# Attention stage: in each of the twelve steps of a turn, TensorE's scores by key go ahead of its scores by query

## The chip, the cores and the metric

The kernel runs on one core of a Trainium2 chip. The time is device microseconds of that core for one execution, the median of several. Clocks of TensorE are given as the share of full speed that was granted.

## The reference

32 sequences of 256 tokens with 128 features go through half a feed-forward, a causal attention and another half feed-forward. The feed-forward is a mixture of eight experts of width 512; each token goes to its best expert if its rank there is below a capacity. What the change touches is the attention, whose core is:

```python
qkv = sn_dense(batch, W_qkv, u_qkv, sigma_qkv)           # 16 heads of 8 features
att = jnp.einsum('bhqd,bhkd->bhqk', q, k) * scale
att = jnp.where(causal[None, None] == 0, big_neg, att)
att = jax.nn.softmax(att, axis=-1)
x = jnp.einsum('bhqk,bhkd->bhqd', att, v)
x = x + sn_dense(x, W_proj, u_proj, sigma_proj)
```

(the residual is the layer's input). Behind it the router's affinities of the second feed-forward are worked out for the same sequence.

## The kernel before, in words

Five stages follow one another: token statistics, routing, experts, attention, experts. The attention (`attention`, from L1039) handles one sequence in a *turn* `b`, from b = -4 to 35, and each turn has NP = 12 *steps*, u = 0 to 11. Every engine walks the same turns and steps with its own list, and the engines are held together by semaphores alone. A sequence passes through several turns: its projections are made three turns ahead, its row maxima one and two turns ahead, its exponentials and outputs in its own turn, and normalisation, projection and the router's part one to four turns behind.

The softmax is made in two passes over the scores, and each step has a piece of both.

- *Scores by query* (`scores_by_query`, L1354 to L1369; called Q below): TensorE makes a 128 x 512 tile of scores with the query on the partitions, adds the causal mask by a matmul with the identity, and leaves it in one of two buffers `at_pp`. VectorE reduces the tile to row maxima (L1609, "the reduce"). Q of a step waits until the reduce of two tiles before is done. The tile belongs to a later sequence: `QUERY_TILES` (L1059) gives steps 0 to 4 the tiles 7 to 11 of sequence b+1 and steps 5 to 11 the tiles 0 to 6 of b+2. Tiles 0 to 3 are two matmuls of 256 columns (L1361) and a mask of 512 (L1363), the others one of 512 (L1366) and a mask of 256 (L1368).
- *Scores by key* (`scores_by_key`, L1371 to L1385; K below): TensorE makes the transposed scores of sequence b into one of two buffers `at_pm`, two matmuls of 256 columns (L1379) or, in every third step, four of 128 (L1383). The row maxima are subtracted within the matmul: they are extra rows of `qs`. ScalarE takes the exponential (L1291) and GpSimd zeroes what lies above the diagonal (L1207). K of a step waits until the exponential of two steps before is done, and K of step 0 also until the maxima have landed in `qs`.

The path of the maxima: after the reduce of tile 11 of sequence b+1 (step 4) GpSimd splits them into three bf16 pieces (L1259 to L1265, step 5), TensorE turns them (L1483, step 8), ScalarE copies them out (L1329) and SyncE's queue writes them into `qs` (L1169, `qs<-at_mt`); step 0 of the next turn uses them. In the same steps other transfers go out: VectorE's last split of the projections (L1642, step 5) is written to DRAM by SyncE's queue (L1164, `at_qkd<-at_part`) and read back by six transfers of ScalarE's queue (L1284, `qs<-at_qkd`, steps 9 to 11) and six of SyncE's (L1176, `kb<-at_qkd`), all of which wait for that write's landing (`part_out`).

On TensorE a step is Q, then K, then in every third step the product with the values (`times_v`, L1400, steps 0, 3, 6, 9), then `small(u)`: transposes and small matmuls. Those that matter below are in step 3 the transposes of `at_xn2` (L1415), which wait for VectorE's normalise of step 2 (L1582); in step 2 the q and k projections (L1418, L1419); in step 8 the turning of the maxima. VectorE's list has, beside one reduce in each step, in steps 10 to 2: two normalises of `at_xa` (L1582, step 10), statistics, the two `at_weight` operations (L1568, step 0), two `at_beats` (L1618, steps 0 and 1) and the two normalises of `at_x` (L1582, step 2).

Of the kernel before, what the change touches and what calls it, by code (L numbers as in the profile page):

```python
# [1038 lines left out]
def attention(nc, m, io, c, x_dram):  # L1039
# [9 lines left out]
    with ctx:  # L1049
# [81 lines left out]
        def wait(eng, s, n, most=None):  # L1131

            n = n if most is None else min(n, most)
            if n > 0:
                eng.wait_ge(s, n)

        def dma_count(b, slots, each=1):

            return lambda k: b * (16 * each // slots) + (16 * each - (k % slots) * (16 * each // slots))
# [210 lines left out]
        def _(pe):  # L1350
            te = nc.tensor

            def turn(b, k, has):
                def scores_by_query(o, v):  # L1354
                    n, s, out = b + o, (k + o) % NQ, pp[v % 2]
                    if v == 0:
                        wait(pe, qk_in[s], dma_count(n, NQ, 12)(s))
                    wait(pe, maxed, n * NP + (v - 1))
                    if v < 4:
                        for w in range(2):  # L1360
                            te.matmul(out[:, w * S:(w + 1) * S], qs[s][0:ROWS, 2 * v + w, 0:P], kb[s][0:ROWS, 2 * v + w, :, 0:P],  # L1361
                                      start=(w == 0), stop=False, skip_group_check=True)
                        te.matmul(out, c.identb[:, :], c.mask[:, :, :].rearrange("p a q -> p (a q)"),  # L1363
                                  start=False, stop=True, skip_group_check=True).then_inc(pre_done, 1)
                    else:
                        te.matmul(out, qs[s][0:ROWS, v - 4, P:S], kb[s][0:ROWS, v - 4, :, :].rearrange("p r q -> p (r q)"),  # L1366
                                  start=True, stop=False, skip_group_check=True)
                        te.matmul(out.rearrange("p (r q) -> p r q", r=2)[:, :, P:S], c.identb[:, :], c.mask[:, 0:2, :],  # L1368
                                  start=False, stop=True, skip_group_check=True).then_inc(pre_done, 1)  # L1369

                def scores_by_key(u):  # L1371
                    s, out, quad, w = k, pm[u % 2], u // 3, u % 3
                    g, r = 4 * (quad // 2), quad % 2
                    if u == 0:
                        wait(pe, m_in[s], dma_count(b, NQ)(s))
                    wait(pe, exped, b * NP + (u - 1))
                    if w < 2:
                        for i in range(2):
                            last = te.matmul(out[:, i * S:(i + 1) * S], kb[s][:, g + 2 * w + i, r, 0:P], qs[s][:, g + 2 * w + i, :],  # L1379
                                             start=True, stop=True)  # L1380
                    else:
                        for j in range(4):
                            last = te.matmul(out[:, j * P:(j + 1) * P], kb[s][:, g + j, r, P:S],  # L1383
                                             qs[s][:, g + j, P:S], start=True, stop=True)
                    last.then_inc(main_done, 1)  # L1385

                def times_v(n, s, quad):
                    half, r = quad // 2, quad % 2
                    out, values = po, vp[s][:, :, :, :].rearrange("p j h w -> p j (h w)")
                    if quad == 0:  # L1390
                        wait(pe, v_out, n + 1)
                        wait(pe, ot_out, n)
                    wait(pe, masked, n * NP + 3 * (quad + 1))
                    for w in range(3):
                        src = pt[3 * quad + w]
                        for i in range(2 if w < 2 else 4):
                            j = 2 * w + i if w < 2 else i
                            cols = S if w < 2 else P
                            at = 32 * (8 * half + 2 * j + r) - 16 * r
                            last = te.matmul(out[32 * j:32 * j + 32, (half + 1) * S - cols:(half + 1) * S],  # L1400
                                             values[:, w // 2, at:at + 32], src[:, i * cols:(i + 1) * cols],
                                             start=(w < 2 and r == 0), stop=(w == 2 and r == 1), skip_group_check=True)
                    last.then_inc(pv_done, 1)
# [81 lines left out]
                        last.then_inc(mt_tr, 1)  # L1485

                for u in range(NP):
                    for o, v in QUERY_TILES[u]:
                        if has(o):
                            scores_by_query(o, v)  # L1490
                    if has(0):
                        scores_by_key(u)
                    if u >= LAG and (u - LAG) % 3 == 2 and has(0):
                        times_v(b, k, (u - LAG) // 3)
                    if u < LAG and (u - LAG) % 3 == 2 and has(-1):
                        times_v(b - 1, (k - 1) % NQ, (NP - LAG + u) // 3)
                    small(u)

            run(turn)
            pe.wait_ge(seen, TPB * B)  # L1500
            te.matmul(ps_n, c.onesb[:, :], c.hots[B % 2][:, 3 * TPB, :], start=True, stop=True).then_inc(counted, 1)
# [245 lines left out]
```

## Time and profile before

| what | value |
|---|---|
| time, median of 3 runs | 1045.26 us (1042.62 to 1045.60) |
| time of the profiled execution | 1035.15 us |
| its span, first to last instruction | 1033.3 us |
| TensorE matmul busy, whole span | 896.4 us (87%) |
| VectorE busy | 724.8 us (70%) |
| ScalarE busy | 607.5 us (59%) |
| GpSimd busy | 682.8 us (66%) |
| TensorE clock granted, mean | 0.955 |

Shares over the whole span mix five stages, so they say little of the attention, which fills about 286 to 860 us of the span. How to read the rows below: a timeline row has start, duration, engine, line, operation, output and input, count, and in brackets the idle time of the engine before it and what ended that. A "q" behind an engine's name (SPq, ACTq) is its sequencer issuing DMAs. Ends of matmuls are modelled, so the distance between starts is what a matmul really takes of TensorE. A turn is recognised by its transposes L1415, one pair in each.

### The profile page before, as it was taken

The page shows a single profiled execution, that of the slowest core. Times are in us where ns is not written, and L with a number is a line of the kernel's source. Part 1 is how long each engine was busy: PE and PEld are TensorE (multiplying, and loading weights), DVE is VectorE, ACT ScalarE, POOL GpSimd, SP SyncE. Part 2 cuts the span into 40 slices and gives each one's busy share as a digit, 9 for nine tenths or more (in the row PEclk, how much of TensorE's full clock was granted, in tenths as well). Part 3 has the DMA queues.
Part 4 walks back from the last instruction along what each step waited for, and adds up shares of the span by engine and source line. Part 5 has one row for each costly group of instructions (what it writes and reads, how often), then busy time and mean ns, then how long its engine had stood idle before and what let it go on. Part 6 is the DMA issues. An engine that isn't in the chain of part 4 may idle for free. (4 is left out here: it accounts for less than half of the span.)

```text
span 1033.3 us, 26499 instructions
## 1 busy us (share of the span) xinstructions
PE 896.4 (87%) x8219; PEld 679.6 (66%) x8219; DVE 724.8 (70%) x2368; ACT 607.5 (59%) x1581; POOL 682.8 (66%) x1247
## 2 busy tenths in 40 slices
PE   5937499999647999999999999999999873999995
PEld 5823399999623566565656666565656542999995
DVE  8879745444237889899998989998898845444441
ACT  2637366666313666676666666666666651766662
POOL 7709668643023678888888888888887773355554
PEclk9999799999958999999999999999999985999998
DMA  7450022223145544446354554545454102222220
GB/s 214 128 173 1 17 69 67 69 66 64 40 79 106 122 96 101 115 94 122 95 116 101 109 108 97 121 95 117 95 115 97 39 24 61 60 67 67 64 59 21
DMA packets 127407, 89.72 MB, mean 87 GB/s; under 512 B 14305, under 2 KB 117910, under 8 KB 127270
## 3 DMA queue, kind: packets, MB, share of 16 engines
q1 hardware_dynamic: 103078, 52.69, 22.8%
q10 hardware_dynamic: 15488, 17.74, 7.7%
q0 software_dynamic: 8704, 17.60, 6.6%
q8 instruction: 70, 1.15, 0.5%
q14 instruction: 67, 0.55, 0.2%
HBM read 52.23 MB, written 35.47 MB: 85 GB/s over the span
## 5 line engine op out<-in xcount | busy, mean ns | idle before, releaser
L1291 ACT ACTIVATE at_pt<-at_pm 128x512 f32<-128x512 f32 x384 | 228.5, 598 | 117.9 <-PE at_pm L1379 84.2
L1609 DVE TENSOR_REDUCE at_mx<-at_pp 128x2 f32<-128x512 f32 (+1 forms) x384 | 259.5, 678 | 44.7 <-PE at_pp L1368 37.1
L1207 POOL TENSOR_SCALAR_AFFINE_SELECT at_pt<-at_pt 128x256 f32<-128x256 f32 (+1 forms) x384 | 187.8, 493 | 57.4 <-ACT at_pt L1291 54.1
L925 ACT ACTIVATE e_ht<-e_ps_h,b1t 128x128 f32<-128x128 f32 x576 | 164.8, 370 | 98.2 <-PE e_ps_h L954 98.2
L964 PE MATMUL e_ps_y<-w,e_ht 128*128 x1152 | 159.2, 282 | 0.0
L954 PE MATMUL e_ps_h<-e_xnt,e_w1own 128*128 128x128 f32 x1152 | 154.8, 279 | 1.4 <-issue 1.4
L954 PEld LDWEIGHTS e_ps_h<-e_xnt,e_w1own 128*128 128x128 f32 x1152 | 143.0, 195 | 1.6 <-issue 1.6
L964 PEld LDWEIGHTS e_ps_y<-w,e_ht 128*128 128x128 f32 x1152 | 140.0, 192 | 1.7
L1011 DVE SCALAR_TENSOR_TENSOR e_y<-e_ps_y,e_x 128x256 f32<-128x256 f32 x72 | 30.6, 425 | 155.7 <-PE e_ps_y L964 155.7
L888 POOL DMA_INDIRECT out_dram<-e_y,e_x x72 | 73.6, 1022 | 86.4 <-DVE e_y L1011 74.8
L1400 PE MATMUL at_po<-at_pt,vp 128*32 128x256 f32 (+1 forms) x2048 | 109.8, 332 | 1.6 <-POOL at_pt L1207 1.6
L1366 PE MATMUL at_pp<-kb,qs 96*128 96x512 bf16 x256 | 100.1, 391 | 8.3 <-DVE at_mx L1609 7.3
L1379 PE MATMUL at_pm<-qs,kb 128*128 128x256 bf16 x512 | 97.6, 272 | 8.6 <-DMA qs<-at_mt 7.4
L855 POOL DMA_INDIRECT e_x<-rows,gidx x72 | 68.8, 955 | 54.8 <-DVE e_y L1011 32.3
L1400 PEld LDWEIGHTS at_po<-at_pt,vp 128*32 128x32 f32 x2048 | 53.4, 109 | 50.5 <-issue 21.9
L1253 POOL DMA_INDIRECT buckets<-at_x,at_to x64 | 65.5, 1023 | 20.0 <-issue 19.3
L1379 PEld LDWEIGHTS at_pm<-qs,kb 128*128 128x128 bf16 x512 | 48.2, 97 | 45.9 <-DMA qs<-at_mt 11.8
L1214 POOL DMA_INDIRECT at_xa<-x,place x64 | 66.0, 1032 | 11.7 <-issue 11.2
L1368 PE MATMUL at_pp<-mask,identb 128*128 128x256 bf16 x256 | 70.8, 276 | 0.0
L1005 DVE COPY e_w1own<-w 128x512 f32 x144 | 62.3, 438 | 8.7 <-issue 5.1
L1361 PE MATMUL at_pp<-kb,qs 96*128 96x256 bf16 x256 | 50.7, 280 | 7.3 <-DMA kb<-at_qkd 7.1
L1366 PEld LDWEIGHTS at_pp<-kb,qs 96*128 96x128 bf16 x256 | 24.7, 96 | 41.7 <-DVE at_mx L1609 29.3
(327 smaller groups left out, 1788.6 us busy)
## 6 DMA issues: line engine op xcount, KB each, us to landing
at_qkd<-at_part SPq DMA_DIRECT2D x64, 192.0 KB, 3.0
kb<-at_qkd SPq DMA_DIRECT2D x64, 96.0 KB
qs<-at_qkd ACTq DMA_DIRECT2D x64, 96.0 KB
e_x<-buckets SPq DMA_DIRECT2D x72, 66.0 KB, 1.9
x<-e_y SPq DMA_DIRECT2D x36, 128.0 KB, 1.8
rows<-ts_x ACTq DMA_DIRECT2D x16, 264.0 KB, 3.0
ts_x<-in_x_dram SPq DMA_DIRECT2D x16, 256.0 KB, 3.5
x_by_token<-at_xa SPq DMA_DIRECT2D x32, 128.0 KB
```

What stands on the lines that cost most here:

```text
L855: pool.indirect_dma_start(x_row[s][:, j % 2, :], None, rows, bass.IndirectOffsetOnAxis(ap=c.gidx[:, j:j + 1], axis=0)).then_inc(x_in[s], 16)
L888: pool.indirect_dma_start(y_dram, bass.IndirectOffsetOnAxis(ap=to, axis=0), y_row[s][:, j % 2, :], None, bounds_check=T - 1, oob_is_err=Fa ...
L925: last = a.activation(hid_t[j % NB][:, f, :], ps_h[j % NB][:, f, :], ACT.Gelu, bias=c.b1t[:, ds(e, 1), f])
L954: last = te.matmul(ps_h[j % NB][:, f, :], w1_own[j % NB][:, f * P:(f + 1) * P], xn_t[(j // 2) % NX][:, j % 2, :], start=True, stop=True, s ...
L964: last = te.matmul(out, hid_t[j % NB][:, f, :], c.w2[:, ds(e, 1), f, :].rearrange("p a d -> p (a d)"), start=False, stop=(f == FC - 1))
L1207: g.affine_select(out=tile, in_=tile, compare_op=ALU.is_ge, fill=0.0, base=0, pattern=[[0, n], [1, P]], channel_multiplier=-1).then_inc(ma ...
L1291: a.activation(pt[u % RING][:, :], pm[u % 2], ACT.Exp, scale=SCALE).then_inc(exped, 1)
L1366: te.matmul(out, qs[s][0:ROWS, v - 4, P:S], kb[s][0:ROWS, v - 4, :, :].rearrange("p r q -> p (r q)"), start=True, stop=False, skip_group_c ...
L1368: te.matmul(out.rearrange("p (r q) -> p r q", r=2)[:, :, P:S], c.identb[:, :], c.mask[:, 0:2, :], start=False, stop=True, skip_group_check ...
L1379: last = te.matmul(out[:, i * S:(i + 1) * S], kb[s][:, g + 2 * w + i, r, 0:P], qs[s][:, g + 2 * w + i, :], start=True, stop=True)
L1400: last = te.matmul(out[32 * j:32 * j + 32, (half + 1) * S - cols:(half + 1) * S], values[:, w // 2, at:at + 32], src[:, i * cols:(i + 1) * ...
L1609: v.tensor_reduce(out, src, axis=AX.X, op=ALU.max).then_inc(maxed, 1)
```

## The change

The two calls change places within a step; nothing else does. No operation, wait or buffer is added or removed.

```diff
                 for u in range(NP):
+                    if has(0):
+                        scores_by_key(u)
                     for o, v in QUERY_TILES[u]:
                         if has(o):
                             scores_by_query(o, v)
-                    if has(0):
-                        scores_by_key(u)
                     if u >= LAG and (u - LAG) % 3 == 2 and has(0):
                         times_v(b, k, (u - LAG) // 3)
```

## Rows read from the trace of the kernel before

**Rows 1.** The page's costliest groups: VectorE's reduce

```profile
L1609 DVE TENSOR_REDUCE at_mx<-at_pp 128x2 f32<-128x512 f32 (+1 forms) x384 | 259.5, 678 | 44.7 <-PE at_pp L1368 37.1
```

**Rows 2.** Waits, 430 to 800 us: us in total, times, longest

```profile
DVE at_mx L1609 <- PE at_pp L1368: 23.7, 42, 0.7
```

**Rows 3.** Busy time in 600 to 700 us: PE, PEld, DVE, ACT, POOL, granted clock, DMA

```profile
600.00:700.00 100.00, 95.56 (x980) 60.94 (x978) 90.95 (x277) 66.30 (x145) 84.92 (x182) 1.00 0.50 107
```

**Rows 4.** Timeline, VectorE's stretch of one turn, from step 10's reduce to L1415

```profile
616.54 0.69 DVE L1609 TENSOR_REDUCE at_mx<-at_pp 128x2 f32<-128x512 f32 x1 [0.73 <-PE at_pp L1368]
...
622.46 0.64 POOL L1207 TENSOR_SCALAR_AFFINE_SELECT at_pt<-at_pt 128x512 f32<-128x512 f32 x1
622.68 0.82 DVE L1582 SCALAR_TENSOR_TENSOR at_xn<-at_x 128x128 f32<-128x128 f32 x2
...
623.57 0.44 PE L1415 MATMUL at_mi<-ident,at_xn 128*128 128x128 f32 x2 [0.36 <-DVE at_xn L1582]
```

**Rows 5.** Timeline, TensorE before that: L1415, then step 10's Q and K, step 11's Q, step 0's K

```profile
606.97 0.44 PE L1415 MATMUL at_mi<-ident,at_xn 128*128 128x128 f32 x2 [0.19 <-DVE at_xn L1582]
...
616.01 0.39 PE L1366 MATMUL at_pp<-kb,qs 96*128 96x512 bf16 x1
...
616.35 0.38 PE L1379 MATMUL at_pm<-qs,kb 128*128 128x256 bf16 x2
...
616.56 0.38 PE L1366 MATMUL at_pp<-kb,qs 96*128 96x512 bf16 x1
...
617.63 0.38 PE L1379 MATMUL at_pm<-qs,kb 128*128 128x256 bf16 x2
```

**Rows 6.** Timeline, the maxima's transfer (SPq) and its neighbour's first two issues (ACTq), same turn

```profile
614.75 0.81 SPq L1169 DMA_DIRECT2D qs<-at_mt  x1
...
615.27 1.02 ACTq L1284 DMA_DIRECT2D qs<-at_qkd  x2
```

**Rows 7.** Timeline, the same in another turn; then K of step 0, then L1415

```profile
697.80 0.81 SPq L1169 DMA_DIRECT2D qs<-at_mt  x1
...
698.30 0.71 ACTq L1284 DMA_DIRECT2D qs<-at_qkd  x2
...
701.67 0.39 PE L1379 MATMUL at_pm<-qs,kb 128*128 128x256 bf16 x2 [0.83 <-DMA qs<-at_mt]
...
706.53 0.44 PE L1415 MATMUL at_mi<-ident,at_xn 128*128 128x128 f32 x2
```

**Rows 8.** Timeline, a third such turn: transfer, K of step 0

```profile
416.57 0.81 SPq L1169 DMA_DIRECT2D qs<-at_mt  x1
...
420.78 0.39 PE L1379 MATMUL at_pm<-qs,kb 128*128 128x256 bf16 x2 [1.17 <-DMA qs<-at_mt]
```

**Rows 9.** Timeline, GpSimd's split, VectorE's L1642, SyncE's write, turn of rows 6

```profile
610.81 0.21 POOL L1259 CAST at_mp<-at_mx 128x32 bf16<-128x32 f32 x1
610.86 0.71 DVE L1642 TENSOR_TENSOR at_part<-at_rest,at_part 128x512 bf16<-128x512 f32 x1
...
611.59 1.30 SPq L1164 DMA_DIRECT2D at_qkd<-at_part  x2
```

**Rows 10.** Timeline, the same three in the turn of rows 7

```profile
693.74 0.21 POOL L1259 CAST at_mp<-at_mx 128x32 bf16<-128x32 f32 x1
693.90 0.68 DVE L1642 TENSOR_TENSOR at_part<-at_rest,at_part 128x512 bf16<-128x512 f32 x1
...
694.61 1.31 SPq L1164 DMA_DIRECT2D at_qkd<-at_part  x2
```

**Rows 11.** VectorE, 430 to 800 us, by line: duration ns min/median/max

```profile
L1568 DVE SCALAR_TENSOR_TENSOR at_weight<-at_aff,at_amax,down x44: 209/229/544, 438.6 to 785.6; 128x8 f32<-128x8 f32 x44
...
L1582 DVE SCALAR_TENSOR_TENSOR at_xn<-at_x x44: 332/394/718, 441.3 to 788.7; 128x128 f32<-128x128 f32 x44
```

**Rows 12.** Timeline, L1415 of two turns, 26 turns apart

```profile
375.80 0.44 PE L1415 MATMUL at_mi<-ident,at_xn 128*128 128x128 f32 x2
...
805.25 0.44 PE L1415 MATMUL at_mi<-ident,at_xn 128*128 128x128 f32 x2 [0.36 <-DVE at_xn L1582]
```

## The prediction, made before the changed kernel was built

> **What bounds the kernel now.** I read the page first, then the attention's busy time by window, then the waits, then the timeline of single turns. The page's costliest group is the reduce, 384 times 0.68 us [rows 1]. In the steady part TensorE is busy 96%, VectorE 91%, GpSimd 85%, at full clock [rows 3]. Neither of the first two is a bound by itself: each waits for the other, VectorE's reduce for Q 23.7 us in 430 to 800 us [rows 2], TensorE for the normalise in the turns of rows 4 and 5 0.36 and 0.19 us [rows 4, 5].
>
> The timeline says where. A turn is a loop of two stretches. In the first VectorE has no gap: from step 10's reduce, which starts when step 10's Q is there (VectorE had been idle 0.73 us), through reduces, `at_xa`, `at_weight` and `at_beats`, to the normalise of `at_x`; TensorE's L1415 starts as it ends, 623.57 - 616.54 = 7.03 us [rows 4]. In the second TensorE has no gap: from L1415 to the next step 10's Q, 9.57 us from 606.97 to the reduce at 616.54 [rows 4, 5]. Together 16.6 us. Over the 26 turns from 375.80 to 805.25 a turn takes 16.52 us on average [rows 12].
>
> A third path runs beside this: the maxima's transfer. It is issued 7.78 us after L1415 (606.97 to 614.75 [rows 5, 6]), and K of step 0 waits for it. In most turns K starts 2.88 us after the issue (614.75 to 617.63 [rows 5, 6]) and doesn't wait; in some it comes late, and K starts 3.87 us [rows 7] or 4.21 us [rows 8] after it. From a late K on TensorE runs without a gap to L1415, 701.67 to 706.53 = 4.86 us [rows 7]; today that costs little, since VectorE would hold L1415 until nearly then anyway.
>
> **The change part by part.** The work is the same; what changes is who starts when.
>
> *K's price.* Step 10's K takes 616.56 - 616.35 = 0.21 us, step 10's Q 616.35 - 616.01 = 0.34 us [rows 5].
>
> *Q later.* Between L1415 in step 3 and step 10's Q lie six K's today (steps 4 to 9), and seven with the change. So step 10's reduce starts 0.21 us later after L1415: 9.78 us instead of 9.57. If VectorE's stretch stays, a turn grows by 0.21 us. The cover that VectorE's other reduces have isn't lost: it waits only at some steps, and each later tile has more than 0.21 us of queue in front of it.
>
> *Q's waits.* Where Q waits for the reduce, in steps 2 and 3, K now goes first into the gap. It gives nothing back: what ends the stretch is VectorE's normalise, and TensorE waits longer at L1415 instead.
>
> *K earlier.* Exponentials start 0.34 us earlier where ScalarE is free, GpSimd's maskings too. K waits for the exponential of two steps back, which is early by as much; queued behind a waiting K are now Q and all that follows, but by the timeline each exponential is over in time.
>
> *K of step 0.* Here the order matters. Its wait for the maxima now has step 0's Q behind it, which today runs while the transfer is under way. With an early landing K would start at 617.4 instead of 617.6, and there is slack in steps 1 to 3. With a late one, Q's 0.34 us goes behind K, onto the gapless path: 4.86 + 0.34 = 5.20 us from K to L1415.
>
> *Will the landing be late?* The rows separate the two kinds. The neighbour queue's first transfers start 0.52 us after the maxima's issue in the early case [rows 6] and 0.50 us in the late one [rows 7]: when their data get in front, the small transfer stands behind them. They start when the write of `at_part` has landed, and that was issued 3.16 us ahead of the maxima's in the early case (611.59 to 614.75 [rows 6, 9]) and 3.19 in the late one (694.61 to 697.80 [rows 7, 10]). The 0.03 us are VectorE's L1642, 0.71 against 0.68 us: short where GpSimd's L1259 had begun 0.16 us before it, long where it had begun 0.05 before [rows 9, 10]. With the change step 5's masking starts as soon as its exponential is done, and GpSimd's earlier work of steps 2 to 4 is out of the way sooner; I get L1259 about 0.14 us earlier, so about 0.19 before L1642. That is the late kind. So I expect late landings in most turns instead of five or so.
>
> The Trainium skill, "DMA: Bandwidth & Descriptors", section "Queues, rings and completion order", says that each DMA engine goes round its queues packet by packet. By that rule a small transfer that is second in line pays for a packet of its neighbour; the rows agree, with about 1 us or more for the late kind. It would not say which of the two comes first, and the sum doesn't rest on it.
>
> *Sum.* A late turn takes 7.78 (L1415 to issue) + 3.87 (issue to K) + 5.20 = 16.85 us, against 16.52: +0.33 us, times 26 = 8.6 us. VectorE's stretch is 16.52 - 9.57 = 6.95 us on average, so its path, 9.78 + 6.95 = 16.73, lies just under it. The four turns before 375.80 I estimate at 0.34 each for Q behind a waiting K, and 0.9 together for landings that come later there too: 2.3 us. The last turn with tiles adds 0.3. Total 8.6 + 2.3 + 0.3 = 11.2 us. The profiled execution of 1035.15 us would become about 1046. It lies 10.1 us below the median of the runs, which no row explains; I add the same amount to the median: 1045.3 + 11.2, 1056 us.
>
> *Bounds.* Late landings lie between 3.87 and 4.21 us: the second makes 0.34 x 26 = 8.8 us more, so +20. If the late ones came a little sooner, 3.7 us, VectorE's path would be the bound, 16.73, and the sum 8. Below that lie the rivals.
>
> **The rivals.**
>
> *Early landings as now, VectorE's stretch unchanged.* Then 0.21 us in about 21 turns and 0.34 in the five that are late today, 4.4 + 1.7, and 1.5 at the start: +7.6, 1053 us. For it: the two kinds are 0.03 us apart. Against: the shift I expect has one direction.
>
> *Faster: VectorE's stretch shrinks.* The two `at_weight` operations take 209 ns at best and up to 544, the normalise of `at_x` 332 and up to 718 [rows 11]. The pair of normalises takes 0.82 us in rows 4 and runs into GpSimd's masking; twice 0.33 would be 0.66, and with the overlap of two that follow each other about 0.60. I take each turn to hold one normalise 0.22 us too long and one `at_weight` 0.21 (0.43 instead of 0.21). The maskings of steps 0 and 2 come about 0.65 and 0.86 us earlier against VectorE with the change, which would take them out of the way of both: 6.95 - 0.43 = 6.52, a turn of 16.30, 0.22 less than now, 5.7 us over 26 turns, less 1.5 lost at the start: 1041 us. It decides from the point where VectorE gains more than the 0.21 us of K and landings stay early; with late landings the gain is hidden behind the third path. The Trainium skill, "GPSIMD Engine Reference", section "1. Specifications", says that GpSimd shares its SBUF interfaces with VectorE and contends with VectorE operations of two SBUF inputs; these are such operations and the reduce from PSUM isn't, and the trace agrees. The gain itself is worked out from the rows alone.
>
> *No change.* Early landings and half of that gain, about 0.2 us a turn, against K's 0.21: 1045 to 1047 us.
>
> **How the numbers follow.** Late landings in most turns 0.55 (1056); early, stretch unchanged 0.20 (1053); faster 0.13 (1041); no change 0.12 (1046). Slower is the first two, 0.75; same 0.12; faster 0.13, where "same" is within 0.3%, about what a measurement of this kernel can tell from no change. The range leaves out the faster case and the far end of late landings (4.2 us in every turn): 1043 to 1064.
>
> **What would show it.** In the profile after: the distance from L1415 to step 10's reduce is 9.78 instead of 9.57; K of step 0 has an idle time ended by `qs<-at_mt` in most turns and starts 3.8 to 4.2 us after its issue; the write of `at_part` comes 3.19 us or more ahead of it; from K to L1415 5.2 us, L1415 without idle time. TensorE's idle time before Q for the reduce is gone or smaller. If L1415 still waits for L1582 in most turns, VectorE is the bound and one of the rivals holds; the durations of `at_weight` and of the normalise then tell which. I would be wrong outright if the 9.57 us didn't grow, or if K were held by exponentials.

## The result and the profile after

| | the kernel before | the change |
|---|---|---|
| time, median of 19 runs each | 1044.21 us (1041.90 to 1046.49) | 1047.17 us (1044.73 to 1051.90) |
| ratio | | 1.0031, 95% interval 1.0019 to 1.0044; +3.0 us between the medians |
| profiled execution, span | 1033.3 us | 1045.0 us |
| first experts' stage, TensorE's L954 first to last start | 143.6 us | 151.1 us |
| second experts' stage, the same | 141.3 us | 143.9 us |
| attention, first L1411 to the first L954 behind it | 590.1 us | 590.5 us |
| TensorE's stretch / VectorE's stretch, mean of 25 turns | 9.58 / 6.96 us | 9.75 / 6.79 us |

The forecast was 1056, slower; it is slower, by a quarter of what I said. The two profiled spans differ by 11.7 us, of which the attention has 0.4. The rest lies in the experts' stages, which the change doesn't touch:

```profile
L954 PE MATMUL e_ps_h<-e_xnt,e_w1own x576: 269/275/567, 129.0 to 280.1; 128*128 128x128 f32 x192
...
L954 PE MATMUL e_ps_h<-e_xnt,e_w1own x576: 274/275/423, 885.3 to 1029.2; 128*128 128x128 f32 x192
```

(The change, TensorE's first expert matmul in the first and the second experts' stage: duration min/median/max in ns, then first and last start.) In the profile of before they run from 128.2 to 271.8 and from 876.6 to 1017.9 us. By these times the two profiles come from different chips. On the chips where the kernel before takes 1044 to 1046 us every profiled kernel has 150 to 151 and 144 to 145 us there, on those where it takes 1034 to 1036 every one has 142 to 144 and 141 to 142. That accounts for a thing that the prediction left open: the profiled execution of before, 10 us below its median, has the stage times of the second kind. I call them the slower and the faster chips. They don't differ everywhere. In each of the five profiles from slower chips ScalarE stands idle once for 9.3 to 10.0 us early in the first experts' stage, and the first 64 starts of L954 span 23.5 to 24.3 us; the profiles from faster chips have no such wait and 15.3 to 17.1 us. The other 512 span 126.77 us in all twenty profiles. In the second stage the other 512 span 129.3 to 129.4 us against 126.77. In the change's profile that wait is:

```profile
142.54 1.14 ACT L925 ACTIVATE e_ht<-e_ps_h,b1t 128x128 f32<-128x128 f32 x4 [10.04 <-remote]
```

("remote" is a release whose origin the trace doesn't have, so the cause isn't shown.) Of two spans from different chips only the attention can be compared.

Read against the groups of before. The page's reduce [rows 1], the waits in 430 to 800 us [rows 2] with those for the maxima's transfer, and the busy time in 600 to 700 us [rows 3]:

```profile
L1609 DVE TENSOR_REDUCE at_mx<-at_pp 128x2 f32<-128x512 f32 (+1 forms) x384 | 261.3, 682 | 56.1 <-PE at_pp L1368 46.9
```

```profile
DVE at_mx L1609 <- PE at_pp L1368: 29.0, 55, 0.7
...
PE at_pm L1379 <- DMA qs<-at_mt: 6.6, 6, 1.3
...
PE at_mi L1415 <- DVE at_xn L1582: 5.8, 15, 0.5
```

```profile
600.00:700.00 100.00, 93.94 (x972) 60.87 (x977) 90.07 (x278) 64.83 (x145) 85.86 (x183) 1.00 0.47 107
```

VectorE waits 5.3 us more for Q than before, as a longer stretch of TensorE would make it. This view puts 6 waits of TensorE's matmuls down to the maxima; counted turn by turn TensorE is idle for over 0.4 us ahead of step 0's K in 11 of 25 turns, not in most. The timeline of a usual turn, from L1415 through step 10's reduce and VectorE's normalises to the next L1415 [rows 4, 5]:

```profile
632.52 0.44 PE L1415 MATMUL at_mi<-ident,at_xn 128*128 128x128 f32 x2 [0.34 <-DVE at_xn L1582]
...
642.26 0.69 DVE L1609 TENSOR_REDUCE at_mx<-at_pp 128x2 f32<-128x512 f32 x1 [0.74 <-PE at_pp L1368]
642.87 0.80 DVE L1582 SCALAR_TENSOR_TENSOR at_xn<-at_xa 128x128 f32<-128x128 f32 x2
...
648.08 0.65 DVE L1582 SCALAR_TENSOR_TENSOR at_xn<-at_x 128x128 f32<-128x128 f32 x2
...
648.78 0.44 PE L1415 MATMUL at_mi<-ident,at_xn 128*128 128x128 f32 x2 [0.29 <-DVE at_xn L1582]
```

642.26 - 632.52 = 9.74 us, where before had 9.57. From the reduce to L1415 it is 648.78 - 642.26 = 6.52 us, against before's 7.03 [rows 4]. Eight of the 25 turns have 6.51 or 6.52; I call them plain. Two of VectorE's lines in 430 to 800 us say why [rows 11]:

```profile
L1568 DVE SCALAR_TENSOR_TENSOR at_weight<-at_aff,at_amax,down x46: 210/219/383, 431.8 to 795.8; 128x8 f32<-128x8 f32 x46
```

```profile
L1582 DVE SCALAR_TENSOR_TENSOR at_xn<-at_x x46: 335/360/552, 434.3 to 798.4; 128x128 f32<-128x128 f32 x46
L1582 DVE SCALAR_TENSOR_TENSOR at_xn<-at_xa x44: 336/514/1011, 445.3 to 792.7; 128x128 f32<-128x128 f32 x44
```

In plain turns of before the two `at_weight` took 0.21 and 0.43 us and the two normalises of `at_x` 0.56 and 0.34; now they take 0.22 and 0.22, 0.38 and 0.34. That is the gain of the "faster" rival. But the third line is new: normalises of `at_xa` of 1009 ns. In six of 25 turns VectorE's stretch is 7.37 us for that reason:

```profile
658.52 0.69 DVE L1609 TENSOR_REDUCE at_mx<-at_pp 128x2 f32<-128x512 f32 x1 [0.74 <-PE at_pp L1368]
...
659.10 0.42 POOL L1207 TENSOR_SCALAR_AFFINE_SELECT at_pt<-at_pt 128x256 f32<-128x256 f32 x1
659.13 1.53 DVE L1582 SCALAR_TENSOR_TENSOR at_xn<-at_xa 128x128 f32<-128x128 f32 x2
659.48 0.31 POOL L1227 TENSOR_TENSOR at_rest_a<-at_aff,at_pieces 128x16 f32<-128x16 f32 x1
...
659.75 0.17 POOL L1246 CAST at_to<-at_spot_of 128x2 int32<-128x2 f32 x1
...
659.88 0.62 POOL L1207 TENSOR_SCALAR_AFFINE_SELECT at_pt<-at_pt 128x512 f32<-128x512 f32 x1
...
665.89 0.44 PE L1415 MATMUL at_mi<-ident,at_xn 128*128 128x128 f32 x2 [0.46 <-DVE at_xn L1582]
```

GpSimd runs four operations without a gap, VectorE's pair takes 1.53 us instead of 0.80, and L1415 comes 0.85 us later. The third kind is the late landing, as in [rows 7]:

```profile
442.70 0.81 SPq L1169 DMA_DIRECT2D qs<-at_mt  x1
443.19 0.70 ACTq L1284 DMA_DIRECT2D qs<-at_qkd  x2
...
446.53 0.39 PE L1379 MATMUL at_pm<-qs,kb 128*128 128x256 bf16 x2 [1.30 <-DMA qs<-at_mt]
...
451.64 0.44 PE L1415 MATMUL at_mi<-ident,at_xn 128*128 128x128 f32 x2
```

K starts 3.83 us after the issue, and from there it is 451.64 - 446.53 = 5.11 us to an L1415 without idle time. In nine of 25 turns K comes more than 3.3 us after the issue, but only in five does L1415 follow without idle time, and in two of these VectorE's normalise ends no sooner. Over the 26 turns [rows 12] nothing is left of it all, 815.12 - 385.46 = 429.66 us against 429.45:

```profile
385.46 0.33 PE L1415 MATMUL at_mi<-ident,at_xn 128*128 128x128 f32 x1
```

```profile
815.12 0.44 PE L1415 MATMUL at_mi<-ident,at_xn 128*128 128x128 f32 x2 [0.35 <-DVE at_xn L1582]
```

### The profile page after: what moved, and what is told of

Same layout as the page of the kernel before. It is cut to its first block and busy times, and to the rows that moved or that the text cites. A ratio compares the mean times of both kernels' runs of the same rounds, so it can differ in the third digit from the quotient of the medians.

```text
span 1045.0 us, 26466 instructions
## 1 busy us (share of the span) xinstructions
PE 895.2 (86%) x8186; PEld 684.2 (65%) x8219; DVE 719.5 (69%) x2368; ACT 595.1 (57%) x1581; POOL 682.4 (65%) x1247
## 5 line engine op out<-in xcount | busy, mean ns | idle before, releaser
L1291 ACT ACTIVATE at_pt<-at_pm 128x512 f32<-128x512 f32 x384 | 225.3, 596 | 83.8 <-PE at_pm L1379 58.1
L954 PE MATMUL e_ps_h<-e_xnt,e_w1own 128*128 128x128 f32 x1152 | 158.0, 281 | 6.3 <-issue 6.0
L954 PEld LDWEIGHTS e_ps_h<-e_xnt,e_w1own 128*128 128x128 f32 x1152 | 144.9, 197 | 8.1 <-issue 8.0
L1379 PE MATMUL at_pm<-qs,kb 128*128 128x256 bf16 x512 | 100.0, 277 | 14.0 <-DMA qs<-at_mt 9.7
L1214 POOL DMA_INDIRECT at_xa<-x,place x64 | 64.4, 1006 | 11.7 <-issue 11.2
L1379 PEld LDWEIGHTS at_pm<-qs,kb 128*128 128x128 bf16 x512 | 39.6, 98 | 49.3 <-DMA qs<-at_mt 25.6
L1000 DVE TENSOR_SCALAR e_xn<-e_x 128x128 f32<-128x128 f32 x144 | 51.4, 362 | 0.3
```

The source lines that it names most:

```text
L954: last = te.matmul(ps_h[j % NB][:, f, :], w1_own[j % NB][:, f * P:(f + 1) * P], xn_t[(j // 2) % NX][:, j % 2, :], start=True, stop=True, s ...
L1291: a.activation(pt[u % RING][:, :], pm[u % 2], ACT.Exp, scale=SCALE).then_inc(exped, 1)
```

## The experiments

The table has every run; each ratio is to the kernel before on the same chip, timed in turns with it. T and V are TensorE's and VectorE's stretches (T as in nearly all turns, V the mean of 25 turns, steps 10 of `b` = 3 to 27), then the time of these 25 turns from L1415 to L1415, the turns in which K of step 0 starts over 3.3 us after the maxima's issue (late) and those with a normalise of `at_xa` over 0.8 us (long). All but the ratio come from one profiled execution.

| kernel | ratio (95% interval) | T | V | 25 turns | late | long |
|---|---|---|---|---|---|---|
| *slower chips* | | | | | | |
| the change, result | 1.0031 (1.0019, 1.0044) | 9.74 | 6.79 | 413.5 | 9 | 6 |
| change_again | 1.0041 (1.0020, 1.0063) | 9.74 | 6.84 | 414.7 | 6 | 7 |
| before_masks | 0.9989 (0.9979, 1.0000) | 9.57 to 10.5 | 6.74 | 415.1 | 21 | 0 |
| change_masks | 1.0020 (0.9994, 1.0045) | 9.74 to 11.1 | 6.43 | 416.5 | 14 | 0 |
| change_rows | 1.0172 (1.0152, 1.0193) | 9.74, once 11.1 | 7.57 | 434.6 | 1 | 0 |
| *faster chips* | | | | | | |
| the kernel before | | 9.57 | 6.96 | 413.4 | 6 | 0 |
| change_third | 0.9972 (0.9956, 0.9987) | 9.74 | 6.72 | 411.5 | 1 | 5 |
| only10 | 0.9996 (0.9983, 1.0010) | 9.79 | 6.73 | 413.1 | 6 | 0 |
| not10 | 0.9958 (0.9945, 0.9972) | 9.52 | 6.81 | 408.3 | 2 | 0 |
| k1to9 | 0.9958 (0.9945, 0.9972) | 9.52 | 6.88 | 410.2 | 7 | 0 |
| not0 | 0.9993 (0.9981, 1.0005) | 9.74 | 6.77 | 412.8 | 4 | 6 |
| change_delay | 0.9963 (0.9948, 0.9978) | 9.74 | 6.66 | 410.0 | 3 | 1 |
| before_delay | 1.0009 (0.9996, 1.0022) | 9.57, twice 9.8 to 10.1 | 6.91 | 412.7 | 3 | 0 |
| change_late | 0.9975 (0.9965, 0.9985) | 9.74 | 6.63 | 409.3 | 6 | 0 |
| change_late_again | 0.9961 (0.9946, 0.9977) | 9.74 | 6.61 | 408.7 | 8 | 0 |
| before_late | 1.0001 (0.9989, 1.0013) | 9.57 | 6.93 | 412.7 | 14 | 0 |
| change_stats | 1.0051 (1.0033, 1.0069) | 9.74 | 7.00 | 418.6 | 4 | 19 |
| not10_stats | 0.9929 (0.9904, 0.9955) | 9.52 | 6.82 | 408.5 | 14 | 0 |
| not10_delay | 0.9952 (0.9938, 0.9966) | 9.52 | 6.76 | 407.0 | 0 | 0 |
| not10_stats_delay | 0.9893 (0.9878, 0.9907) | 9.52 | 6.59 | 402.6 | 2 | 0 |

A late turn isn't always a late landing. K of step 0 also waits for the exponential of step 10, and in some turns it starts 0.14 us behind that one's end. That holds for one late turn each of the change, change_again, before, before_masks, before_late, change_late, not0, not10, not10_stats and not10_stats_delay, two each of before_delay and change_stats, and three each of k1to9 and change_delay. A turn of change_delay, where two DMA issues on ScalarE's queue take 2.15 us ahead of that exponential:

```profile
548.20 2.15 ACTq L1286 DMA_DIRECT2D qs<-at_qkd  x2
550.45 0.60 ACT L1293 ACTIVATE at_pt<-at_pm 128x512 f32<-128x512 f32 x1 [2.51 <-PE at_pm L1385]
...
551.20 0.38 PE L1381 MATMUL at_pm<-qs,kb 128*128 128x256 bf16 x2 [1.28 <-ACT at_pt L1293]
```

So the change has eight late landings in 25 turns, the kernel before five, change_delay none.

**Which steps carry the price of the order.** The edit names the steps in which K goes first: `(10,)` in only10, all but 10 in not10, all but 0 in not0, `range(1, 10)` in k1to9.

```diff
+                    first = u in (10,)
+                    if first and has(0):
+                        scores_by_key(u)
                     for o, v in QUERY_TILES[u]:
                         if has(o):
                             scores_by_query(o, v)
-                    if has(0):
+                    if not first and has(0):
                         scores_by_key(u)
```

only10:

> K goes ahead of Q in step 10 alone, everything else as before. Theory (step 10's K is the price: it lengthens TensorE's stretch from L1415 to step 10's reduce by 0.17 to 0.21 us, and nothing else of the change is there to pay it back): the stretch is 9.74 us in every turn, VectorE's stretch stays near 6.95, a turn 16.7, the kernel 4 to 5.5 us slower than before (ratio 1.004 to 1.005). Rival (the loss of the change comes from late landings of the maxima and from VectorE being held, not from K's place): no difference, ratio 1.000 within 0.15%.

not10:

> K goes ahead of Q in every step but 10. Theory: TensorE's stretch is back at 9.57 us, VectorE's stretch short as in the change (6.52 in most turns), so a turn is 0.17 us shorter than in the change: 4 us faster than the change, about 1 us faster than before (ratio 0.998 to 1.000). Rival (late landings and holds make the loss): as slow as the change, ratio 1.003.

k1to9:

> K goes ahead of Q in steps 1 to 9 alone; steps 10, 11 and 0 as before. Theory (three terms: K of step 10 costs 0.17 us, Q of step 0 behind the maxima's transfer costs 0.34 where the landing is late, and earlier exponentials take GpSimd's maskings out of VectorE's way, worth 0.43): the first two are gone and the third stays, TensorE's stretch 9.57 and VectorE's near 6.5, a turn 16.1, 8 to 12 us faster than before (ratio 0.989 to 0.993). Rival (the short VectorE stretch depends on steps 10 and 11 being early too, or holds take it back): 6.9 us as before, ratio 0.999 to 1.001.

not0:

> K goes ahead of Q in every step but 0. Theory: as in the change, but a late landing of the maxima finds Q of step 0 done; in the nine or so late turns L1415 comes up to 0.34 us sooner: 2 to 3 us faster than the change, ratio to before 1.000 to 1.001. Rival (late landings are covered by VectorE's stretch anyway): as the change, 1.003.

T says it plainly: 9.79 with K first in step 10 alone (+0.22), 9.52 with K first everywhere else (-0.05), 9.74 with both (+0.17). So the price is step 10's K, as the prediction had it, less 0.05 which the other steps give back. Yet only10 costs no time (0.9996, the rival of its expectation): its V falls by as much, since the later start frees the second normalise of `at_xa`, 0.34 instead of 0.57 us. The pair in only10, then in not10:

```profile
535.94 0.60 DVE L1585 SCALAR_TENSOR_TENSOR at_xn<-at_xa 128x128 f32<-128x128 f32 x2
```

```profile
532.12 0.83 DVE L1585 SCALAR_TENSOR_TENSOR at_xn<-at_xa 128x128 f32<-128x128 f32 x2
```

not10 and k1to9 keep that hold, in most turns, and shed the price. They are 0.42% faster than before: not10 beat its expectation of 0.998 to 1.000, k1to9 fell short of 0.989 to 0.993, since its V is 6.88 and not near 6.5. K ahead in step 0 is not what costs: not0 has the change's T, its six long turns and no better time than change_third.

**GpSimd's maskings.** The masking works on 8 of 128 columns (what of the mask is left out stands in the expectation):

```diff
-                        tile = pt[u % RING][:, :].rearrange("p (h q) -> p h q", h=n)[:, :, 0:P]
+                        tile = pt[u % RING][:, :].rearrange("p (h q) -> p h q", h=n)[:, :, 0:8]
```

before_masks:

> The order of before; GpSimd's masking covers 8 of the 128 query columns of each block, so most of the causal mask is left out and each masking is shorter. It takes GpSimd's long operations out of VectorE's way. Theory (GpSimd's maskings hold VectorE's two-input operations, 0.6 us a turn): VectorE's stretch falls from 6.95 to about 6.3 us, TensorE's stays 9.57, a turn 15.9, 15 to 17 us faster than before (ratio 0.984 to 0.986). Rival (the long durations are not GpSimd's doing): stretch 6.9, ratio 0.999 to 1.000.

change_masks:

> The change's order with the same short maskings (most of the causal mask left out). Theory: with no holds left, only the prices of the order remain: TensorE's stretch 9.74, VectorE's about 6.3 as in the other order, so 0.17 us a turn and 4 to 5 us in all slower than the old order with short maskings (ratio to before 0.988 to 0.990), plus up to 1.5 for late landings. Rival (the change gains or loses elsewhere too): as fast as the old order with short maskings, within 1 us, or over 7 us slower.

The holds go in both: `at_xa` 0.34 and 0.36 us, `at_weight` 0.22, `at_x` 0.34, V down to 6.3 us where nothing else binds. So the held time of these operations is the maskings'. But neither kernel got faster, against 0.984 to 0.990 expected: K of step 0 is now late in 21 of 25 turns of before_masks and in 14 of change_masks, and in most of them it decides L1415. before_masks, K of step 0, VectorE's normalises, L1415:

```profile
545.33 0.62 DVE L1582 SCALAR_TENSOR_TENSOR at_xn<-at_xa 128x128 f32<-128x128 f32 x2
...
546.96 0.39 PE L1379 MATMUL at_pm<-qs,kb 128*128 128x256 bf16 x2 [0.98 <-DMA qs<-at_mt]
...
550.60 0.60 DVE L1582 SCALAR_TENSOR_TENSOR at_xn<-at_x 128x128 f32<-128x128 f32 x2
...
551.79 0.44 PE L1415 MATMUL at_mi<-ident,at_xn 128*128 128x128 f32 x2
```

VectorE is done at 551.20 and L1415 starts at 551.79, 4.83 us behind K without a gap; in change_masks that distance is 5.11. T also grew in many turns of both, which I didn't follow up. The pair shows the holds' cause and that the transfer is the next bound; it doesn't price the order.

**Early landings, by moving the read-backs.** ScalarE's first read-back goes from step 9 to step 10, the rest to step 11:

```diff
-                    if u in (9, 10, 11) and has(3):
-                        q_rows(b + 3, (k + 3) % NQ, (k + 1) % 2, u - 9)
+                    if u in (10, 11) and has(3):
+                        q_rows(b + 3, (k + 3) % NQ, (k + 1) % 2, u - 10)
+                    if u == 11 and has(3):
+                        q_rows(b + 3, (k + 3) % NQ, (k + 1) % 2, 2)
```

change_rows:

> The change, with ScalarE's read-back of the projections issued in steps 10 and 11 instead of 9 to 11, so that it can't get in front of the maxima's transfer. Theory (late landings cost up to 0.27 us in the turns where K of step 0 comes late and L1415 has no idle time, and those turns are a minority): K starts 2.5 us after the maxima's issue in all turns, and the kernel is 1 to 3 us faster than the change (ratio to before about 1.000). Rival (my forecast: late landings set the time of the change): more than 5 us faster than the change, ratio 0.995.

The landings became early (K 2.5 us after the issue) and the kernel 1.7% slower. The timeline of ScalarE (ACTq its sequencer, issuing):

```profile
516.84 2.21 ACTq L1284 DMA_DIRECT2D qs<-at_qkd  x4
519.15 0.60 ACT L1291 ACTIVATE at_pt<-at_pm 128x512 f32<-128x512 f32 x1 [2.10 <-issue]
```

An exponential stands 2.10 us behind four DMAs on the same engine, K and the masking behind it. So this edit has a price of its own, far above what it was to measure, and it settles nothing about the landings.

**Early or late landings, without that price.** Waits on a count already reached, in SyncE's list: four ahead of the write of `at_part` (change_delay, before_delay, not10_delay) make the read-backs later, three ahead of the maxima's transfer (change_late, before_late) make that one later.

```diff
                     wait(sp, part_done, n + 1)
+                    for _ in range(4):
+                        wait(sp, part_done, n + 1)
```

change_delay:

> The change, with four more waits on the already reached count of `part_done` in SyncE's list, ahead of the write of `at_part`: a small delay of the read-backs, nothing else. If the kind of landing is set by the read-backs coming in front of the maxima's transfer, and four waits give 0.05 us or more, K of step 0 starts 2.5 us after the issue in every turn, and the landings are out of the account. If late landings are what the change costs, the turns that they bound lose 0.2 to 0.4 us each and the whole comes 2 to 4 us lower, about the time before (0.998 to 1.001). If they only fill slack in front of VectorE, whose stretch is 6.52 us in good turns and 7.37 in some, the time stays as the change's, 1.003 to 1.004, and the long normalises are the cost.

before_delay:

> The kernel before, with the same four waits in SyncE's list. Its five late landings go, if the delay is enough. They ended TensorE's wait at L1415 hardly later than VectorE did, so I expect 0.998 to 1.000. A larger gain would mean that late landings cost the kernel before more than its profile shows; a time above 1.002 would mean that later read-backs themselves cost something, and then the run of the change with the same waits is to be read against this one.

change_late:

> The change, with three more waits on the already reached count of `mt_out` in SyncE's list, ahead of the maxima's transfer: its issue comes some 0.17 us later, behind the read-backs, so that the landing should be late in every turn, as the prediction had it. In the change late turns have a stretch of 6.6 to 6.9 us from the reduce to L1415; with 0.17 more, turns of 16.5 to 16.85 us, K of step 0 to L1415 5.11 us without a gap. If late landings cost what the prediction says (turn 16.85), about 8 us over the kernel before: 1.007 to 1.009. If they hide in front of VectorE, 1.003 to 1.004 as the change itself.

before_late:

> The kernel before with the same three waits: landings late in every turn under the old order. K of step 0 to L1415 is then 4.83 us without a gap, 0.28 less than in the change, so this one should hide more of it: turns of 16.4 to 16.6 us and 0.999 to 1.003. The difference from the change with the same waits prices the order under late landings: 0.2 to 0.3 us a turn, 5 to 8 us, if it is the bound in both; near nothing if VectorE is.

Four waits are worth nearly 0.2 us: from the write of `at_part` to the maxima's issue it is mostly 2.94 us in change_delay and 3.13 in change_third, the change itself on a chip of the same kind, and the neighbour's first issue comes mostly 0.73 to 0.81 us behind the maxima's instead of 0.53 to 0.57. Three waits ahead of the maxima's issue make it 0.12 us later (7.85 us behind L1415 instead of 7.73). The landings obey, but not as a switch: change_delay has no late landing and before_delay one, but in change_late the neighbour comes mostly 0.42 to 0.47 us behind, and K starts 2.9 to 3.3 us after the issue in 16 of 25 turns, not 3.5 or more. And the price is small. before_late has 14 late turns and takes the time of before (1.0001). change_late, at 0.9975 below both cases of its expectation, waits for the maxima almost twice as long as the change does by this view (6.6 us there), and V is smaller:

```profile
PE at_pm L1381 <- DMA qs<-at_mt: 12.2, 17, 1.4
```

What shrank V in all three variants of the change with waits is mostly the long turns, five to seven in the change, none or one here. The same turn in change_late:

```profile
500.96 0.69 DVE L1611 TENSOR_REDUCE at_mx<-at_pp 128x2 f32<-128x512 f32 x1 [0.74 <-PE at_pp L1370]
501.54 0.42 POOL L1209 TENSOR_SCALAR_AFFINE_SELECT at_pt<-at_pt 128x256 f32<-128x256 f32 x1
501.57 0.86 DVE L1584 SCALAR_TENSOR_TENSOR at_xn<-at_xa 128x128 f32<-128x128 f32 x2
501.92 0.31 POOL L1229 TENSOR_TENSOR at_rest_a<-at_aff,at_pieces 128x16 f32<-128x16 f32 x1
502.19 0.28 POOL L1248 CAST at_to<-at_spot_of 128x2 int32<-128x2 f32 x1
```

Up to the cast every offset from the reduce is that of the turn at 658.52 within 0.02 us: masking at 0.58, normalise at 0.61, subtraction at 0.96. There the cast took 0.17 us and VectorE's second normalise 1009 ns; here the cast takes 0.28 and the normalise 0.34. One of the two goes first, and when it is GpSimd, VectorE is held through the masking of 128 x 512 behind the cast too. In the result and change_third together 11 turns have a first normalise of 0.59 us or more and a cast of 0.17; all 11 have the 1009 ns. Where the cast takes 0.27 or 0.28, none has. Why waits in SyncE's list decide it isn't shown.

**Is it the waits or the chip?** By then the change had been timed on slower chips alone, its variants with waits on faster ones. So both went to one chip:

change_again (slower chip):

> The change itself, timed beside the others on the same chip: ratio 1.003 as before.

change_third:

> The change itself once more, beside its twin with three more waits, on one chip. So far the change was timed on chips on which the kernel before takes 1044 to 1046 us, and its variants with waits on chips on which it takes 1034 to 1036, so that the chip could be what differs. If the waits make the difference, this is 1.002 to 1.005 again, with five to eight turns of 7.37 us; if the chip does, it is 0.996 to 0.999 with none or one.

change_late_again:

> The change with three more waits ahead of the maxima's transfer, again, on the same chip as the change. If the waits make the difference, 0.996 to 0.999 as before, with none or one of the long turns, 4 to 8 us below the change; if the chip does, it agrees with the change within 0.2%.

It was mostly the chip: the change itself is 0.9972 there, *faster* than before, and change_late_again 0.9961, inside each other's intervals. By the profiles the waits do remove the long turns (5 to 0, 2.8 us over 25 turns), but timed it is 1.1 us between medians, within the uncertainty of both. So the comparisons of this section hold among the runs on the same kind of chip only, and the sign of the change depends on the chip: 1.0031 and 1.0041 in two timings on slower chips, 0.9972 in the one on a faster chip. What the profiles show of the difference, result against change_third: late turns 9 against 1, five of which bind and cost 0.1 to 0.4 us each (1.3 us); from the first L1411 to the first L1415 75.0 against 73.3 us; long turns 6 against 5. In change_again 15 turns have GpSimd's masking 0.65 us or more behind the reduce instead of 0.58, in 12 of them with normalises of 0.34 and 0.49. The kernel before was not profiled on a slower chip with full masks, so how much of its 10 us more there lies in the attention is inferred alone: the experts' stages carry 7.5 and 2.6, about all of it. What in the chip moves the attention isn't shown either.

**The holds, by moving the victims.** The normalises of `at_xa` go from ahead of the statistics of `at_x` to behind them; by the timeline that is 0.4 us later, still in step 10 and not behind step 11's, as the expectations put it. In the second kernel K is also first in all steps but 10:

```diff
-                    if u == 10 and has(4):
-                        wait(dve, rstd1, b + 5)
-                        wait(dve, xt_tr, (b + 3) * TPB)
-                        normalise(xn[k % 2], xa[k % 2], xn_done)
```

(the same four lines then stand ahead of the block of `if u == 11 and has(-1):`)

change_stats:

> The change, with the two normalises of `at_xa` taken behind the first statistics of step 11 instead of ahead of step 10's ones, so that they start some 0.7 us later against GpSimd's masking. In the change the second of them takes 493 ns in most turns and 1009 in six or seven, VectorE's stretch 6.5 and 7.37 us. If the 1009 ns come from GpSimd's row of operations that begins at the moment of the first normalise, the six long turns go (5 us less, 0.997 to 1.000); if holds only move from one operation to the next, the stretch stays between 6.5 and 7.4 us, with long operations elsewhere, and the time within 0.2% of the change's, 1.002 to 1.005. The projections of step 2 get their rows 0.7 us later, which by the profile has room.

not10_stats:

> K ahead of Q in every step but 10, and the normalises of `at_xa` behind the first statistics of step 11. K first in every step but 10 gave 0.9958, with the second normalise held at 571 ns in most turns and VectorE's stretch at 6.77 us. If the move frees it (340 ns), the stretch is 6.55 us, a turn 16.1 instead of 16.3, 0.2 us x 26 = 5 us less: 0.991. If another operation is held in its place, 0.995 to 0.997. Late landings could take part of the gain: K of step 0 started 2.75 us after the issue there.

In the change the move made the long turns the rule, 19 of 25, where the expectation had them go:

```profile
538.04 0.69 DVE L1609 TENSOR_REDUCE at_mx<-at_pp 128x2 f32<-128x512 f32 x1 [0.74 <-PE at_pp L1368]
538.62 0.42 POOL L1207 TENSOR_SCALAR_AFFINE_SELECT at_pt<-at_pt 128x256 f32<-128x256 f32 x1
538.65 0.47 DVE L1515 BATCH_NORM_STATS2 at_bn<-at_x 128x6 f32<-128x128 f32 x2
539.00 0.22 POOL L1227 TENSOR_TENSOR at_rest_a<-at_aff,at_pieces 128x16 f32<-128x16 f32 x1
539.04 1.16 DVE L1582 SCALAR_TENSOR_TENSOR at_xn<-at_xa 128x128 f32<-128x128 f32 x2
539.16 0.26 POOL L1246 CAST at_to<-at_spot_of 128x2 int32<-128x2 f32 x1
...
539.38 0.62 POOL L1207 TENSOR_SCALAR_AFFINE_SELECT at_pt<-at_pt 128x512 f32<-128x512 f32 x1
```

The pair now takes 1.16 us, the second of it 908 ns, again held through the masking of 512. It prices the hold: V 7.00 against change_third's 6.72, 0.28 x 26 = 7.3 us, and 1.0051 - 0.9972 of 1035 us is 8.2. With K last in step 10 the same move does the opposite, the pair takes 0.44 and 0.34 us, V is 6.44 in plain turns, and late landings take the place of the hold in 14 turns (V up to 7.5). Take those away too:

not10_delay:

> K ahead of Q in every step but 10, with four more waits ahead of the write of `at_part`, so that landings are early. Without them this order gave 0.9958 and late landings were few. TensorE's stretch 9.52, VectorE's 6.77 us: 0.995 to 0.997 if late landings were not what was left there, 0.993 or less if VectorE's holds go too.

not10_stats_delay:

> K ahead of Q in every step but 10, the normalises of `at_xa` behind step 11's first statistics, and the four waits ahead of the write of `at_part`. Without the waits this was 0.9929, with 10 late turns of 6.6 to 7.5 us in VectorE's stretch and 6.44 in the others. If late landings are what the long ones are, all turns come to 9.52 + 6.44 = 15.96 us against some 16.3: 0.3 us x 26 = 8 us less, 0.985 (0.983 to 0.988). If the holds move when the landings do, 0.990 to 0.995.

Alone the four waits give not10 nothing (0.9952 against 0.9958). With the move they give 0.36%, from ratios on two chips of the faster kind, and not10_stats_delay beats both kernels: 1023.91 us (four executions) against 1034.14, 0.9893 (0.9878 to 0.9907). A turn of it, L1417 being L1415 and L1614 the reduce:

```profile
587.29 0.44 PE L1417 MATMUL at_mi<-ident,at_xn 128*128 128x128 f32 x2 [0.41 <-DVE at_xn L1587]
...
596.81 0.69 DVE L1614 TENSOR_REDUCE at_mx<-at_pp 128x2 f32<-128x512 f32 x1 [0.52 <-PE at_pp L1370]
597.81 0.70 DVE L1587 SCALAR_TENSOR_TENSOR at_xn<-at_xa 128x128 f32<-128x128 f32 x2
```

T 9.52, V 6.44 us, 15.96 together against 16.54 of before's mean. My expectation of 0.985 had every turn like this; the mean V is 6.59, 0.15 us x 26 = 4 us short of it. It was not timed on a slower chip.

## Why the prediction was wrong

*TensorE's stretch.* Right: 9.57 became 9.74 in 23 of 25 turns; I had 9.78, leaving out 0.05 that K ahead in the other steps gives back (not10).

*Late landings in most turns.* Wrong, the step that failed first, and with it the 8.6 us of the sum. They came in eight of 25 turns on the chip of the result and in one on a faster one, and only five decided L1415. The argument from 0.03 us was too fine. I had L1259 start 0.19 us ahead of L1642 and L1642 take 0.68 us, with the write 3.19 us ahead of the maxima's transfer. In the result L1642 takes 0.68 or 0.69 us and the write comes 3.18 or 3.19 us ahead in 12 of 25 turns, and of these seven are late and five aren't. In change_third L1259 starts 0.34 us ahead in 23 of 25 turns, L1642 then takes 0.74 or 0.75 us, and the write comes 3.12 or 3.13 us ahead: the early kind. The neighbour's issue does come 0.48 to 0.50 us behind in most late turns and 0.51 or more in most early ones, but which it is changes from turn to turn and from chip to chip.

*A late turn's price.* Where a late landing did bind, the turn took 9.74 + 6.61 to 6.93 = 16.35 to 16.67 us, not 16.85: K to L1415 5.11 instead of 5.20, K 3.5 to 3.8 us after the issue instead of 3.87, the issue 7.73 us behind L1415 instead of 7.78. before_late shows the other half: under the old order 14 late turns cost nothing that the time shows, because VectorE is there hardly sooner.

*VectorE's stretch stays.* Wrong, and the larger error: the sum took 6.95 us over from before and left the gain to a rival at 0.13. In plain turns it is 6.52, just the rival's figure, from the two operations that it named. A change that moves K by 0.34 us moves every masking behind it, and V was made of those overlaps.

*What no case had.* The long turns. For the 25 turns the account is: all plain, 25 x (9.74 + 6.52) = 406.5 us, 6.9 less than before's 413.4; six long ones give back 6 x 0.85 = 5.1; five late ones 1.3; smaller holds and two longer TensorE stretches about 0.6. Together +0.1, as in the table.

*The sum.* +11.2 was made of 8.6 + 2.3 + 0.3 for late turns; the profile has +0.2 over 26 turns, +1.5 ahead of them and -1.2 behind them, +0.4 over the attention. The timed +3.0 us is more than this one execution shows; its executions spread from 1044.7 to 1051.9 us, and how many long and late turns the others had isn't known. The range, 1043 to 1064, held the time only because it spanned all rivals but the faster one; that is no merit of the mechanism. By mechanism it came out between "no change" (1045 to 1047: early landings and half of the gain) and slower; half of the gain was lost, but to the long hold and not as I had it. The sign held on the chip of the result, with some luck; on the faster chip it was wrong. "Same" and "faster" deserved most of the chance.

The Trainium skill, "GPSIMD Engine Reference", section "1. Specifications", has GpSimd and VectorE contend for SBUF where VectorE has two SBUF inputs. The runs agree (short maskings free all of those operations; the reduces from PSUM take 0.68 us on average in before and in the change alike), but it gives no size, and here the size was everything: 0.2 us in one overlap, 0.67 in another, by who goes first.

## What to carry to other kernels

Where two engines pass each other the lead in a loop, sum both stretches after the edit, not the edited one alone; a shift of 0.3 us on one engine re-times every overlap of GpSimd's operations with VectorE's, and that can outweigh the work moved. Look for the victims first (operations with two SBUF inputs beside a row of GpSimd operations without a gap), then place them, and only then reorder TensorE. And before a variant is compared with the change, time both on one chip: here the change's own effect moved by 0.6% between chips, more than the effect itself.

## What the runs showed of the hardware that I had not expected

- A normalise of 0.34 us (128 x 128, both inputs in SBUF) takes 0.49 to 0.72 us beside one masking and 0.90 to 1.01 when GpSimd's next two operations go ahead of it; with offsets equal within 0.02 us both outcomes occur, 0.34 or 1.01.
- A small transfer issued 0.5 us ahead of its neighbours on another queue lands so that its reader starts 2.5 to 3.8 us after the issue. Bringing the neighbour closer, to 0.42 to 0.47 us (change_late), did not make that later: mostly 2.9 to 3.3. With the neighbour 0.67 us or more behind (the four kernels with four waits) two landings in 100 turns were late.
- Chips differ by 10 us in 1040 in the experts' stages, and 7 to 8 of them are one wait of ScalarE early in the first stage, behind which 512 matmul starts span 126.77 us on both kinds; what makes the wait isn't shown.
- A DMA issue on ScalarE's queue takes 0.31 us at the median in before and 0.33 in the change, but two in a row now and then take 2.0 to 2.3 us (at 648.41 in before, 773.56 in the change, 548.20 in change_delay), and the exponential behind them on that engine starts after both: it stood idle 2.1 to 2.5 us ahead of it.
- Four waits on a semaphore count already reached delay SyncE's next issue by 0.18 to 0.19 us (3.16 to 2.98 us in before, 3.13 to 2.94 in the change), three by 0.12, which makes them a fine adjustment without free buffers or changed work.
